# Silu in a burst on ScalarE, norm scales by exp of log, and a later copy of each state's last column

## The reference

```python
xz = jnp.einsum('btd,pd->btp', x, W_xproj)          # 64 + 16 + 16 columns: dt_raw, B, C
dt = jax.nn.softplus(jnp.einsum('btr,dr->btd', dt_raw, W_dt) + b_dt)
dA = jnp.exp(dt[..., None] * A)                      # A = -exp(A_log)
dBx = dt[..., None] * Bm[:, :, None, :] * x[..., None]
h = dA_t * h + dBx_t                                 # scan over t
y = jnp.einsum('bds,bs->bd', h, C_t)                 # sum over the 16 states
x = _layernorm(x + (y + Dp * x))
h = jax.nn.silu(gate) * up                           # gate, up: x @ w.T / 127
x = _layernorm(x + jnp.einsum('bsh,dh->bsd', h, wd))
```

## Time and profile before

| what | value |
|---|---|
| median of 3 runs | 2001.36 us (1996.81 to 2002.66) |
| span of the profiled execution | 2000.0 us |
| busy share of the span: PE, DVE | 88%, 91% |
| busy share of the span: ACT, POOL | 78%, 85% |
| mean granted TensorE clock | 0.953 of full |
| DMA queue q1 | 214.40 MB, 32.7% of 16 engines' span |

### The profile page before, as it was taken

The page is one execution under the profiler, slowest core; times in us unless marked ns, Lnnn a source line. Parts: engine busy times, 40 slices in busy tenths (PEclk is TensorE's granted clock), DMA queues, the critical chain, the costliest instruction groups (busy, mean ns, idle before and its releaser), DMA issues.

```text
span 2000.0 us, 37094 instructions
## 1 busy us (share of the span) xinstructions
PE 1766.9 (88%) x11048; PEld 1388.2 (69%) x11048; DVE 1828.2 (91%) x2285; ACT 1568.7 (78%) x2924; POOL 1701.9 (85%) x779
## 2 busy tenths in 40 slices
PE   6788989988899988889888989889989888899886
PEld 3666777676777767777666767667767667777764
DVE  4899999999999999999999999999999999999994
ACT  6878878788877878787788787888777787787862
POOL 5998888988888988889888888988889888889880
PEclk9899999999999999999999999999999999999999
DMA  7233233233233233233233333233333332332300
GB/s 242 89 109 118 94 119 123 90 122 117 86 119 126 87 119 117 96 117 127 85 122 104 110 117 115 97 120 98 117 117 101 111 116 87 117 133 70 122 12 21
DMA packets 116565, 215.35 MB, mean 108 GB/s; under 512 B 11153, under 2 KB 45554, under 8 KB 116466
## 3 DMA queue, kind: packets, MB, share of 16 engines
q1 hardware_dynamic: 116466, 214.40, 32.7%
HBM read 195.48 MB, written 18.87 MB: 107 GB/s over the span
## 4 chain that ended last, share of the span: by engine, by line
PE 51%; issue 19%; DVE 15%; ACT 11%; POOL 2%; DVEq 1%; ACTq 0%; DMA 0%; POOLq 0%; SPq 0%
PE p_o L1005 16%; PE p_y L960 9%; DVE h L705 8%; PE p_m L992 6%; PE p_da L934 5%; PE p_c L943 3%; PE p_m L906 3%; DVE hid L749 3%; PE p_m L914 3%; ACT p_da L539 2%; PE p_m L982 2%; ACT da_k L539 2%; ACT L539 2%; DVE silu_g L743 2%; DVE h L713 1%
## 5 line engine op out<-in xcount | busy, mean ns | idle before, releaser
L422 POOL TENSOR_TENSOR h<-h,c_bc 128x1024 f32<-128x1024 f32 x352 | 832.2, 2368 | 147.6 <-ACT h_carry L525 119.8
L412 POOL TENSOR_TENSOR ub<-u,b_bc 128x1024 f32<-128x1024 f32 x320 | 756.8, 2370 | 0.1
L960 PE MATMUL p_y<-ident,h 128*128 128x128 f32 x4096 | 535.6, 278 | 3.3 <-DVE h L713 2.2
L960 PEld LDWEIGHTS p_y<-ident,h 128*128 128x128 f32 x4096 | 479.9, 144 | 38.5 <-issue 16.4
L539 ACT ACTIVATE p_da<-dt,neg_a 128x512 f32<-128x512 f32 x640 | 432.1, 682 | 86.7 <-DVE h L705 82.8
L705 DVE TENSOR_TENSOR_SCAN h<-p_da,ub 128x512 f32<-128x512 f32 x320 | 380.4, 1210 | 37.9 <-ACT p_da L539 27.4
L705 DVE TENSOR_TENSOR_SCAN h<-p_da,h_carry,ub 128x512 f32<-128x512 f32 x320 | 399.2, 1269 | 11.0 <-ACT p_da L539 10.3
L553 ACT ACTIVATE ub_t<-u_t,bc_t 128x256 f32<-128x256 f32 x768 | 344.9, 497 | 27.7 <-issue 26.9
L1005 PE MATMUL p_o<-wt_down,hid 128*128 128x256 f32 x1536 | 354.7, 381 | 11.8 <-DVE hid L749 8.6
L934 PE MATMUL p_da<-ident,ub_t 128*128 128x128 f32 x1536 | 242.7, 295 | 132.6 <-DVE h L705 131.8
L1005 PEld LDWEIGHTS p_o<-wt_down,hid 128*128 128x128 f32 x1536 | 284.4, 190 | 67.8 <-issue 29.6
(11 more groups left out here) (101 smaller groups left out, 1819.6 us busy)
## 6 DMA issues: line engine op xcount, KB each, us to landing
c_bc<-bc_rows_dram SPq DMA_DIRECT2D x352, 256.0 KB, 4.9
b_bc<-bc_rows_dram SPq DMA_DIRECT2D x128, 512.0 KB, 5.3
x_in<-in_L_attn_x SPq DMA_DIRECT2D x32, 512.0 KB, 3.5
b_bc<-bc_rows_dram SPq DMA_DIRECT2D x64, 256.0 KB, 3.1
out_x<-res_n SPq DMA_DIRECT2D x32, 512.0 KB, 3.3
bc_rows_dram<-bc_rows SPq DMA_DIRECT2D x32, 64.0 KB, 1.6
hid<-in_L_ffn_w_gate SPq DMA_DIRECT2D x1, 768.0 KB, 5.0
hid<-in_L_ffn_w_up SPq DMA_DIRECT2D x1, 768.0 KB, 6.8
```

Source lines behind the costliest of these rows:

```text
L412: nc.gpsimd.tensor_tensor(ub[:, i % UB_SLOTS, :, :], u[:, par, :, :], b_bc[:, i:i + 1, :].broadcast_to([P, DH, T]), ALU.mult).then_inc(s_u ...
L422: nc.gpsimd.tensor_tensor(h[:, s % H_SLOTS, :, :], h[:, s % H_SLOTS, :, :], c_bc[:, i:i + 1, :].broadcast_to([P, DH, T]), ALU.mult).then_i ...
L960: ins = nc.tensor.matmul(p_y_tok[:, k, q * P:(q + 1) * P], h[:, s % H_SLOTS, q, k * P:(k + 1) * P], ident[:, :], start=(s == SUM_ORDER[0] ...
```

## The change

- `silu_of` on DVE and Tanh on ACT go. ACT takes Silu of the gate straight into `hid`, and `hidden` multiplies `hid` by up in place. Gate and up are separate jobs: all six gates come first, two banks of `p_m` in turn, in units 9 and 10, and the six Silus stand together on ACT, between two loads of the activation table. The ups and hiddens follow in units 10 to 15.
- The norm scale is exp(-0.5 ln(var + eps)) on ACT, and one DVE instruction makes the shift. POOL has no norm work. Softplus and the norms use one table set that has both exp and log, loaded by hand (`exp_table`).
- `carry` of state s is issued in zone 0 of unit s+1, behind the jobs of that zone, no longer at the end of unit s.
- The K states are 2, 6, 9, 10, 14, 15 (before 2, 5, 8, 10, 12, 15), still six; the POOL states change places, still eleven. The decays of the K states 6, 10, 14 and 15 are written two units ahead, with semaphores of their own. x1 and the second norm's output are made a quarter at a time. SP starts each broadcast by the unit in which its buffer is freed. Most entries of `AT` move.

```diff
-POOL_STATES = (0, 2, 3, 4, 5, 8, 9, 10, 11, 12, 14)
+POOL_STATES = (0, 1, 2, 3, 4, 7, 9, 10, 11, 13, 14)
+CARRY_LAG = 1
+CARRY_ZONE = 0
...
-    "gate_up": (9, 2), "tanh": (9, 0), "silu": (10, 0), "hidden": (10, 1),
+    "silu0": (9, 0), "silu1": (9, 1), "silu2": (9, 1), "silu3": (9, 1), "silu4": (9, 3), "silu5": (10, 1),
...
-K_STATES = (2, 5, 8, 10, 12, 15)
+K_STATES = (2, 6, 9, 10, 14, 15)
+DA_LEAD = {6: 2, 10: 2, 14: 2, 15: 2}
...
-            def norm_scalars(c):
-
-                wait(pool, s_ln_in, 2 * c)
-                nc.gpsimd.tensor_tensor(rstd[:, :, :], var_eps[:, :, :], neg_half[:, :, :],
-                                        ALU.pow).then_inc(s_rstd, 1)
...
-            def tanh_of(c, j):
+            def silu(c, j, bank=None):
                 act.wait_ge(s_gate_ps, NH * c + (j + 1))
-                nc.scalar.activation(tanh_g[:, :], p_m[:, 0, :], ACT.Tanh,
-                                     scale=0.5 / (QUANT * X1_SCALE)).then_inc(s_tanh, 1)
-
...
+                nc.scalar.activation(hid[:, j, :], p_m[:, j % 2, :] if bank is None else bank, ACT.Silu,
+                                     scale=1.0 / (QUANT * X1_SCALE)).then_inc(s_silu, 1)
+
+            def exp_table():
+                nc.scalar.preload_act_table_set("natural_log_exp_and_others")
+
+            def norm_log(call, c1, c2, k=slice(0, 2)):
+                wait(act, s_mean[0], c1)
+                wait(act, s_mean[1], c2)
+                nc.scalar.activation(log_var[:, k, :], mean_var[:, k, :, 1], ACT.Ln,
+                                     bias=eps[:, :]).then_inc(s_log_var, 1)
+
+            def norm_exp(call, k=slice(0, 2)):
+                act.wait_ge(s_log_var, call)
+                nc.scalar.activation(rstd[:, k, :], log_var[:, k, :], ACT.Exp, scale=-0.5).then_inc(s_rstd, 1)
...
-                        if core and par == 0 and zone == 1:
-                            carry(c, s)
...
+                        if zone == CARRY_ZONE:
+                            cq, sq, pq = unit_at(c, s, -CARRY_LAG, par)
+                            if pq == 0 and (core if s >= CARRY_LAG else prev):
+                                carry(cq, sq)
...
-            def silu_of(c, j):
-                wait(dve, s_hid, NH * c + j)
-                dve.wait_ge(s_tanh, NH * c + (j + 1))
-                nc.vector.scalar_tensor_tensor(silu_g[:, :], tanh_g[:, :], 1.0, p_m[:, 0, :],
-                                               ALU.add, ALU.mult).then_inc(s_silu, 1)
...
+            def gate(c, j):
                 pe.wait_ge(s_x1_lo, c + 1)
...
+                if j >= 2:
+                    pe.wait_ge(s_silu, NH * c + (j - 1))
...
+            def up(c, j):
+                if j >= 2:
+                    pe.wait_ge(s_hid, NH * c + (j - 1))
+                else:
+                    pe.wait_ge(s_silu, NH * c + (NH - 1 + j))
```

More of the change, by code:

```diff
@@ L76, in mamba_ffn_block @@
     NB = N - NK
-    B_RUNS = [[s for s in B_STATES if sum(k < s for k in K_STATES) == r] for r in range(NK)]
-    assert K_STATES[-1] == N - 1 and all(B_RUNS)
+    B_RUNS = [[s for s in B_STATES if sum(k < s for k in K_STATES) == r] for r in range(NK + 1)]
+    B_RUNS = [run for run in B_RUNS if run]
+    RUN_OF = {s: r for r, run in enumerate(B_RUNS) for s in run}
+    NR = len(B_RUNS)
     assert NB % UB_SLOTS == N % H_SLOTS == NK % K_SLOTS == 0
     assert all(sum(AT[f"skip{a}"]) > max(SUM_LAG.values()) for a in range(2))
+    assert all(2 <= DA_LEAD[s] < s and s in K_STATES for s in DA_LEAD)
+    da_at = [s - DA_LEAD.get(s, 1) for s in K_STATES]
+    assert da_at == sorted(da_at)
     sum_at = {s: s + SUM_LAG[s in POOL_STATES] for s in range(N)}
@@ L164, in mamba_ffn_block @@
         p_m = ps("p_m", [P, 2, T])
-        tail_ps = (p_m, p_da)
-        tail_t = (tanh_g[:, :], ub[:, 0, 0, :])
+        tail_ps = [ps_[:, a, :] for ps_ in (p_m, p_da) for a in range(2)]
         p_m_flat = p_m[:, :, :].rearrange("p a t -> p (a t)")
@@ L208, in mamba_ffn_block @@
         s_da = sem("s_da")
+        s_da_k = [sem(f"s_da_k{q}") for q in range(DH)]
         s_scan = sem("s_scan")
@@ L286, in due_at @@
             return lambda job: AT[job] == (s, zone)
-        def tiles(job, s, zone, zones, c, prev, last):
-            for j in range(NH):
-                sixth = 6 * AT[job][0] + 6 // zones * AT[job][1] + TILE_STEP * j
-                slot = sixth // 6
-                if sixth % 6 * zones // 6 == zone:
-                    assert slot < N
-                    if slot == s and prev:
-                        yield c - 1, j
         SMALL_LOADS = 4
@@ L630, in step @@
                             softplus_log(c + 1, 1 - par)
-                        if prev and due("norm1"):
-                            norm1(c - 1)
+                        for k in range(TT):
+                            if prev and due(f"norm1_{k}"):
+                                norm1(c - 1, k)
                         if prev and due("x1_high"):
                             x1_high(c - 1)
-                        for chunk, j in tiles("tanh", s, zone, 2, c, prev, last):
-                            tanh_of(chunk, j)
@@ L637, in step @@
-                        if last and due("norm2"):
-                            norm2(c - 2, c)
+                        if (prev or last) and due("norm_log"):
+                            norm_log(c, c if prev else 0, c - 1 if last else 0)
+                        if (prev or last) and due("norm_exp"):
+                            norm_exp(c)
+                        for j in range(NH):
+                            if prev and due(f"silu{j}"):
+                                silu(c - 1, j)
+                        if prev and due("exp_table"):
+                            exp_table()
@@ L639, in step @@
+                        for k in range(TT):
+                            if last and due(f"norm2_{k}"):
+                                norm2(c - 2, c, k)
                         if nxt and not prev and zone == 0 and s - AT["weights"][0] - 1 in range(WEIGHT_BATCHES):
                             weights_out(s - AT["weights"][0] - 1)
[L641 to L644 removed]
@@ L661, in _ @@
+                for k in range(TT):
+                    norm2(c, c + 3, k)
             over_chunks(act, step, tail)
@@ L1049, in step @@
                             x1_transposed(c - 1, nxt, last)
-                        if nxt and not prev and zone == 1 and s - AT["weights"][0] in range(WEIGHT_BATCHES):
+                        if nxt and not prev and zone == 2 and s - AT["weights"][0] in range(WEIGHT_BATCHES):
                             weights_transposed(s - AT["weights"][0])
-                        for chunk, j in tiles("gate_up", s, zone, 3, c, prev, last):
-                            gate_up(chunk, j)
-                        if zone == 2 and core and s + 1 in K_STATES:
+                        for j in range(NH):
+                            if prev and due(f"gate{j}"):
+                                gate(c - 1, j)
```

319 lines of the change are left out of this document (146 added, 173 removed), and 15 rows, old and new, of the table AT.

## The result

The changed kernel takes 1965.86 us (median of 4 runs, 1959.58 to 1973.62) where the kernel before, on the same chip, takes 2001.82 (1996.81 to 2002.66): ratio 0.9832, 95% interval 0.9804 to 0.986. It is 36 us faster. The prediction said 73 us faster (1929); the time lies inside its range and the direction is right, but half of the gain isn't there. Timed again it took 1964.77 (experiment 9, ratio 0.9826).

What follows compares the result with a forecast made beforehand. VectorE was taken to set the pace, 56.6 us busy of a 60.14 us period. Work 53.1, burst 2.8, C row 0.6 and small waits 1.3 gave 57.8 us, 72.5 less over 31 periods: 1929 us, range 1868 to 1995.

Steps and rivals of the forecast that it cites:

- VectorE's work: VectorE's busy time a chunk: 56.6 us less 3.5 for six `silu_of` of 0.58, so 53.1.
- the burst's wait: Units 9 to 11, six gates and Silus between table loads: VectorE waits 2.8 us a chunk for unit 11's decay.
- the C row: TensorE's C row of unit 6, behind the x1 transposes in unit 7: VectorE's product waits 0.6 us a chunk.
- the small waits: VectorE's remaining waits, read from the old trace: 1.3 us a chunk, 1.2 for decays and 0.1 other.
- Silu and the loads: ScalarE: a Silu takes 0.60 us, as Tanh did; a table switch 1.3 us, without the skill page's 1380 ns drain.
- dt and `x1_low`: VectorE's waits for the softplus log before dt (1.1 us a chunk) and for `x1_high` before `x1_low` (0.5) go.
- GpSimd has room: GpSimd, about 52 us busy of 57.8, has 5.8 us of room a chunk; removing its power gains nothing itself.
- Both at about 0.1 and the difference as nothing: On VectorE, one small `shifts` replaces two small norm inputs: each about 0.1 us, no net cost.
- Rival 1: Burst hidden better, unit 11's decay 1.9 us sooner: period 55.9 us, time 1870 us; chance 0.24.
- Rival 2: TensorE's clock falls before the x1 transposes: 1967 us in half the chunks, 2006 in all; chance 0.17 for a part.
- Rival 3: TensorE's low clock lasts through the burst's gates: up to 64 us a period, 2120 us; slower overall had chance 0.12.
- Rival 4: GpSimd: carry copies of units 8 and 9 stand behind Silus, unit 9's product waits; no separate chance given.

Runs made afterwards that it cites:

- experiment 9: The changed kernel itself timed once more, nothing altered: 1964.77 us.
- experiment 10: Changed kernel plus one unused VectorE instruction ahead of each `hidden`, one operand in PSUM, one in SBUF, as in the removed `silu_of`: 2033.69 us.
- Experiment 16: Kernel before, order kept, its VectorE product of Tanh and gate cut to 8 of 512 columns (most of Silu left out): 1968.35 us.
- Experiment 2: Changed kernel with a plain scaled copy in place of Silu, so both table loads around the six activations fall away: 1919.26 us.
- experiment 3: Changed kernel with the x1 transposes one zone later, behind the C row of unit 6: 1968.23 us.
- experiment 12: Changed kernel with an unused 128x8 power put back on GpSimd each chunk, behind unit 6: 1964.37 us.
- experiment 1: Changed kernel with the carry copy back at the end of its own unit: 1964.5 us.
- experiment 6: Changed kernel with GpSimd's u of the next chunk moved behind its product of unit 4: 1983.89 us.
- experiment 13: Changed kernel with u behind GpSimd's product of unit 4 and the shift's first operand from PSUM (mean left out): 1955.24 us.
- experiment 5: Changed kernel with both VectorE residual instructions one scan later: 1960.48 us.
- experiment 7: Changed kernel with carry copy closing its unit, x1 transposes behind the C row of unit 6, and u behind GpSimd's product of unit 4: 1979.95 us.
- experiment 8: Changed kernel with the three moves of experiment 7 and the residuals one scan later: 1975.03 us.
- experiment 4: Changed kernel plus one unused VectorE instruction ahead of each `hidden`, both operands in SBUF: 2138.43 us.
- experiment 11: Changed kernel with u behind GpSimd's product of unit 4 and the shift as eight one-column `tensor_scalar` instructions with a pointer: 2039.99 us.

## Why the prediction was right in direction and wrong in size

The forecast's period has four terms, and this profile measures each: VectorE's work 53.2 us (forecast 53.1), the burst's wait 2.6 (2.8), the C row 0.9 (0.6), the small waits 6.05 - 2.6 - 0.9 = 2.55 (1.3). The first three are right within 0.3 us. The fourth is off by 1.25 us a chunk, and 31 x 1.25 is 39 of the 45 us by which this execution is above the forecast.

**The step that failed** is the last term of the sum, "1.3 for what stays of the small waits (the 1.2 for decays, and 0.1)"; 2.55 was measured in its place. It holds two mistakes, and they partly overlap.

The first is in the reading of the old trace. Of VectorE's 3.6 us of idle time the prediction names 1.2, 1.1 and 0.5. Of the 0.8 left it keeps 0.1, without a reason. The 0.7 are there: in the middle of the trace, from 100 to 1900 us, the residual waits 12.9 us for the down projection and scans 11.0 for transposes, 0.4 a chunk each. Kept as they stood, the forecast would have been some 20 us higher.

The second is that the prediction took the small waits from the earlier trace rows as they stood and the 3.5 us of work at full length, by "a microsecond off VectorE is worth a microsecond only as long as the others, at 51 to 54, do not come into its way". The shares of busy time, 51 to 54 against 57.8, said that nobody would. But at single places VectorE meets chains of other engines that do not get shorter with its work, and it now comes to them earlier. For the burst experiment 10 shows this, 0.66 against 1.25 us; for the other places it is the reading of the waits. Experiment 10 also gives the size. By the forecast's own terms its period is 53.1 + 3.5 + (2.8 - 0.6) + 0.6 + 1.3 = 60.7 us, or 2019; it took 2033.7, 15 us more. The changed kernel took 1964.8 for 1929, 36 us more. So 15 us are missing with the work in place, and 21 only once it is off.

In the changed kernel, what grew is spread over transposes, `ub`, the residual and issue. Experiment 16 shows the same kind of loss for the old order, where 31 of 89 us came out, but at other places: there the scans behind `silu_of` wait for the refill of `p_da`. In the changed kernel the scans directly behind a `hidden` wait for `p_da` outside the burst in 5 places only, 0.6 us in all; its waits for transposes stand at other scans, most of them directly behind another scan.

Point by point:
- **VectorE's work**: 53.2 a chunk, forecast 53.1. Right.
- **The burst's wait**: 2.6 us (2.8), 10.88 us long (10.3). Right in size; it is two waits, for the first up (1.33 a chunk, which was not named) and for the decay (1.28). The prediction's own chain has the first one: gate 5 ends at 7.7, so the up behind it at about 8.7, and VectorE is at `hidden0` at 6.9. Its 5.4 us for ScalarE ahead of the burst are the load and two pairs each of `ub_t` and `da_k`, as in the trace, where its text says three pairs. Experiment 2: the second load counts in full, the first is all but hidden.
- **Silu and the loads**: 597 ns (600) and 1283 (1280), no drain behind them. The first rows of the burst settle it against the drain of the Trainium skill (ScalarE: Activation LUTs, "What ACT_TABLE_LOAD costs"): 0.02 us pass from a load's end to the next activation.
- **The C row of unit 6**: 0.9 us a chunk (0.6). Right in kind; but taking it away gains nothing (experiment 3).
- **dt and `x1_low`**: their waits are gone, as said. That log and exp lie beside work: they take 0.30 and 0.21 us, and nobody waits.
- **GpSimd has room; the power is worth nothing**: shown by experiment 12.
- **The carry copy worth nothing**: shown by experiment 1.
- **"Both at about 0.1 and the difference as nothing"** for `shifts`: true in the changed kernel (141 ns in the median, none over 0.8 us between the first chunk and the tail), but only since GpSimd waits for dt there. The step missed a mechanism that costs 19 us a unit away (experiments 6 and 13).
- **Rival 1** (burst hidden better) did not happen. **Rival 2** (TensorE's clock) happened in part of the chunks. TensorE stood idle for 1.92 us ahead of the x1 transposes at 699.65, and in the stretch 699 to 706 its granted clock is 0.61 of full in the mean, between its two levels of 1.2 and 2.4 GHz; in that chunk it is 12.5 us from `x1_low` to the scan of unit 11, 1.7 more than in the other. But this costs little. Of 28 chunks in the middle of the run, each taken from 8 us before the start of `x1_low` to the same point of the next, 15 have a granted clock of 1.00 in both the 8 us before and the 8 us behind that start, and VectorE is idle 5.8 us in them, already 1.1 over the forecast; 10 have a lower clock only before it, with 5.9, and 3 also behind it, with 7.8. By these means the low clock costs some 7 us of the run. The mean clock of the whole rose, from 0.953 to 0.966. The time that came out lies in this rival's range (1950 to 1995), but for another reason. **Rival 3** did not happen: gates at 1.00 in the stretch 647 to 654. **Rival 4** did not happen.

What stays open: how the 2.55 us of small waits divide into causes. The waits name the places, but they can't be taken apart by removing one at a time, since most of what was removed came back elsewhere (experiments 3, 5, 7, 8). Experiment 10 has its extra work ahead of the `hidden`s and not where `silu_of` stood, so its 15 and 21 us belong to that placement. Why the clock falls ahead of the burst in some chunks and not in others was not tried.

## What to carry to other kernels

Let the waits in the sum add up to the whole idle time of the pacing engine before any is struck out; a remainder that nobody named is still paid. Then price work that is taken off this engine by what it covers: where a buffer is refilled between two of its instructions, or another engine's chain ends at a fixed time behind it, a short instruction ahead of the wait is partly free, and a wait read from the old trace is only the part that was not covered. One test is cheap and can be made before the change is written: shrink the work in the old kernel and see whether the time follows. When one small wait after another is removed and the time stands still, look at the idle time's sum, not at the list; and check each small two-operand instruction of VectorE for where its operands live and what GpSimd does at that time.

## What the runs showed of the hardware

- A VectorE instruction with both tensor operands in SBUF and a GpSimd instruction hold each other up. A 128x8 one of 139 to 141 ns took 424 in the median, and ended 0.03 us behind GpSimd's (experiment 6); a 128x512 one of 0.66 us took 1307 ns in the mean, and GpSimd's 2.37 became 2.72 (experiment 4). With one operand in PSUM it was never seen: at most 143 ns (experiment 13), and 674 in the mean for 128x512 (experiment 10). The same effect in price: 105 us between experiments 4 and 10, 29 between 6 and 13. The Trainium skill states this (SBUF — State Buffer, "Who interferes with whom"): a VectorE instruction with two SBUF inputs contends with a GpSimd instruction that reads SBUF, and the order of issue decides which of them is held up. The traces agree, with the numbers above. `tensor_scalar` of one column with a pointer was not held up (205 ns in the mean, experiment 11).
- Eight small instructions in place of one in VectorE's loop body raised its wait on its own issue from 9.9 us in 14 places to 53.3 us in 13 (experiment 11). The mechanism was not looked into.
